# A two-layer decoder on one core: weights converted at other places, and a second bank for the turned probabilities

## Chip, core and metric

One core of one Trainium2 chip runs the whole program in one launch. The metric is device microseconds. A core has TensorE (PE in the profile, with PEld for its weight loads), VectorE (DVE), ScalarE (ACT) and GpSimd (POOL), which run their own instruction streams and wait on one another by semaphores, and SyncE (SP), which issues most DMAs. Matmuls and transposes write PSUM, eight banks of 128x512 f32 each.

## What is computed

`x` and `ctx` are (64, 128, 256) f32: 64 tiles of 128 tokens, 8192 tokens of width 256.

```python
x = x + ssm(layernorm(x))                 # layer 0: scan over 128 tokens, 8 heads of 64, state 128
x = x + cross16(layernorm(x), ctx)        #          16 heads, rotary, keys and values from ctx
x = x + recur(layernorm(x))               #          gated recurrence over the 64 tiles
x = x + self_gqa(layernorm(x))            # layer 1: 16 query heads, 4 key/value heads, s + s @ w_o
x = x + cross1(layernorm(x), ctx)         #          one head of width 256, /sqrt(256)
x = x + moe(layernorm(x))                 #          top 2 of 8 experts by sigmoid(logits + bias),
                                          #          each expert's weight a mean over all its tokens,
                                          #          plus one shared MLP of width 256
```

The recurrence's state goes from tile to tile, and one step of it in layer 0 ends before the next begins. The self attention is `softmax(q k^T / 16) v` for each head, over the 128 tokens of a tile. An expert's factor needs the chosen tokens of the whole input, so no expert output is weighted before all 64 tiles are routed.

## The kernel before, in words

**Phases.** The program is cut into phases with a barrier between them: `start` loads and converts layer 0's weights and computes the decays; `layer0` runs 64 tiles; `between` converts layer 1's weights; `layer1` runs 64 tiles; `route` chooses the experts and converts their weights; `experts` does the shared and the chosen MLPs. In a phase every engine has its own code (`block.tensor`, `block.scalar`, ...).

**Weight jobs.** `weights(pre, scratch, jobs)` gives four functions, for SP, PE, ACT and DVE. A job takes 128 rows of a weight: SP loads them into one of 8 stages, PE transposes 128x128 blocks into bank `j % 4` (L314), ACT copies the first part out (a float32r part, or one half of a plain f32 weight), DVE writes what is left of it (the low part, L344 or L346: weight minus the high part). PE waits for DVE three jobs back. A projection `mm3` then takes three matmuls (L188 to L190) of high and low parts. A narrow job is 128x256, two transposes.

**The loop of layer 1.** `pipeline(eng, lag, step)` calls `step(i)` for 64 + lag values of i; inside a step, `b = i - k` names the tile that each stage works on, and the order of the stages in a step is written out by hand, for each engine apart. So one trip through the loop on an engine is one tile's worth of work, put together from tiles up to six apart on PE. Self attention (`s_`) of a tile goes: layer norm (VectorE's statistics and seed, 11 small steps of a square root's inverse on GpSimd, `newton`, L385, VectorE's norm L1816), `s_transpose` (L1573), `s_project` (L188 to L190, 384 columns), the rotation on VectorE (L1823, L1829), `s_turn_qk` (L1584), `s_heads` on ScalarE (L1720), scores of eight heads into banks 2 and 3 (L709, `scores` 0), maximum (L716), exponentials (L726), then the same banks for the other eight heads (`scores` 1). `turn` g (g = 0 to 3) transposes the probabilities of four heads (L745). All four write bank 4. ScalarE takes turns 0 and 2 out of it (L751), VectorE turns 1 and 3 (`take_by_vector`, L756), both into one count, and each turn waits until the one before is taken. `values` (L779) multiplies them by v, and `s_out` (L188) projects. The one-head attention (`d_`): norm on VectorE (L1816), `d_transpose` into bank 5 (L1597), `d_project`, `d_scores` into bank 6, `d_turn`, `d_values`. The router (`g_`): norm, `g_transpose` (L1628) and `g_logits` (L1634) in bank 7.

VectorE's piece between two steps' statistics is where the engines meet: PE's `d_transpose` waits for VectorE's norm of `d`, which waits for GpSimd's steps, which waits for VectorE's residual.

**Blank rows.** The experts' gather reads a table `pair_rows` in HBM of 11,776 rows of 516 words (512 words of zeros, then a token number and weights), which GpSimd fills with blank rows at the head of `layer1` by four DMAs of 5.9 MB (L1937); its `newton` steps stand behind them in its stream.

**Route.** VectorE computes a one-hot table `t_hot` (L2092) and, later, `t_sums` (L2129). PE's first routing matmuls are at L2023 and L2036; in its stream the jobs `w2` (12 narrow ones) stand before L2023, and `w3` (26) between L2023 and L2036.

Of the kernel before, what the change touches and what calls it, by code (L numbers as in the profile page):

```python
# [26 lines left out]
P = 128  # L27
D = 256
DI = 512
NH = 8  # L30
# [4 lines left out]
DH = 16  # L35
# [25 lines left out]
def constant_table():  # L61
# [29 lines left out]
    "start": """  # L91
        dt_loaded small_loaded halved bias_rows_ready bo2_mm start_state bv_hi bv_lo expA_ready
# [13 lines left out]
        r_tfi r_go r_tg r_xo r_store r_a r_b r_d  # L106
    """.split(),
    "between": """
        w1_load0 w1_load1 w1_load2 w1_load3 w1_load4 w1_load5 w1_load6 w1_load7 w1_scaled w1_tr w1_hi w1_lo b_v b_vrow b_gate l1_small
        l1_wg l1_whi l1_wlo  # L110
# [5 lines left out]
        blank_ready blank s_xo s_u s_h s_x3 s_stats s_aggr s_seed s_rs s_xn s_tr s_hi s_lo s_qkv s_qr s_v s_qtr s_kT  # L116
        s_qT s_sc s_max s_exp s_ptr s_pt s_pv s_rec s_rinv s_rtr s_rT s_o s_ohi s_olo s_proj s_x4
# [5 lines left out]
        w2_load0 w2_load1 w2_load2 w2_load3 w2_load4 w2_load5 w2_load6 w2_load7 w2_scaled w2_tr w2_hi w2_lo  # L123
        w3_load0 w3_load1 w3_load2 w3_load3 w3_load4 w3_load5 w3_load6 w3_load7 w3_scaled w3_tr w3_hi w3_lo
# [11 lines left out]
def decoder(nc, args, xo_dram, cum_dram, table, out):  # L136
# [8 lines left out]
    with ExitStack() as stack:  # L145
# [31 lines left out]
        def pipeline(eng, lag, step):  # L177

            for i in range(lag + 1):
                step(i)  # L180
            with eng.Fori(lag + 1, NB) as i:
                step(i)
            for i in range(NB, NB + lag):
                step(i)
# [40 lines left out]
        WORK, WORKR = 11664, 2560  # L225
# [47 lines left out]
        wpos = [0]  # L273

        def wk(n):
            a = work[:, wpos[0]:wpos[0] + n]
            wpos[0] += n
            assert wpos[0] <= WORK, wpos
            return a
# [11 lines left out]
        def weights(pre, scratch, jobs):  # L291
# [7 lines left out]
            def sync(e):  # L299
                for j, (rows_, n, _, _, _) in enumerate(jobs):  # L300
# [107 lines left out]

        layer0_weights = ExitStack()
        w0r = layer0_weights.enter_context(nc.sbuf_tensor("w0r", [P, 6144], F32R))  # L410
        w0p = layer0_weights.enter_context(nc.sbuf_tensor("w0p", [P, 6144], F32))
        w_out = parts_view(w0r, 0, 4, D)
# [15 lines left out]
        for r in range(2):  # L428
# [5 lines left out]
            for g, (wx, wu) in enumerate(ff):  # L434

                jobs0 += [(wx[r * P:(r + 1) * P, :], D, plain(w_rx, g * D + r * P), 1.0, None),
                          (wu[r * P:(r + 1) * P, :], D, plain(w_ru, g * D + r * P), 0.5, None)]
        jobs0 += [(out_proj[r * P:(r + 1) * P, :], DI, to(w_out, r * P), 1.0, nw_row) for r in range(2)]
# [9 lines left out]
        pdt = [work[:, 8192 + 512 * k:8704 + 512 * k] for k in range(4)]  # L448
        cumT = work[:, 10240:10752]
        q_dtT = work[:, 10752:11264]  # L450
# [3 lines left out]
        PAIRS_OF_X = NB // 2  # L454

# [8 lines left out]
        with phase("start") as block:  # L464
            @block.sync
            def _(e):
                e.dma_start(const[:, :], table[:, 0:C_END]).then_inc(S["const_loaded"], 16)
                e.dma_start(dt_stage, in_proj[DI + XBC:DI + XBC + NH, :]).then_inc(S["dt_loaded"], 16)
                w0[0](e)
# [28 lines left out]
            def _(e):  # L498
# [37 lines left out]
                last.then_inc(S["q_dtT"], 1)  # L536
                w0[1](e, range(PAIRS_OF_X, len(jobs0)))

                e.wait_ge(S["bv_lo"], 1)
                e.wait_ge(S["w0_lo"], len(jobs0))  # L540
# [5 lines left out]
                e.wait_ge(S["p_nd"], 1)  # L546
                e.matmul(dt_bank[:, 0:NT], upper, pdt[3], start=True, stop=True).then_inc(S["p_cum"], 1)
                for k in range(0, NT, P):
                    last = e.matmul(bank[6][:, k:k + P], pdt[3][:, k:k + P], upper, start=True, stop=True)
                last.then_inc(S["p_cumT"], 1)  # L550

            @block.scalar
            def _(e):
# [11 lines left out]
                w0[2](e, range(PAIRS_OF_X, len(jobs0)))  # L565
# [5 lines left out]
                e.activation(pdt[3], pdt[1], ACT.Ln, bias=const[:, C_ONE:C_ONE + 1]).then_inc(S["p_act"], 1)  # L571
                e.wait_ge(S["p_cumT"], 1)
# [1937 lines left out]
```

## Time and profile before

| | |
|---|---|
| time, median of 3 runs | 3503.76 us (3502.93 to 3503.86) |
| the profiled execution | 3505.98 us, of which the span is 3504.2 |
| TensorE's granted clock, mean | 0.957 |
| start, layer 0 (64 tiles) | 87.8 us; 1797.70 us |
| between | 16.50 us |
| layer 1 (64 tiles) | 1085.40 us |
| route; experts | 75.90 us; 440.90 us |
| busy: PE, DVE, ACT, POOL | 89%, 79%, 65%, 44% |

The span is what the trace covers, and the execution's own time is 1.8 us longer. The phases add up to the span, since a barrier stands between them. A phase of 64 tiles costs 64 times its period plus a head and a tail.

### The profile page before, as it was taken

How to read it: one execution, taken by the hardware profiler on the slowest of the kernel's cores; microseconds unless marked ns; L12 is line 12 of the kernel's file. 1: busy time of each engine (PE TensorE's matmuls, PEld its weight loads, DVE VectorE, ACT ScalarE, POOL GpSimd, SP SyncE). 2: the span in 40 equal slices, each digit the busy share in tenths (PEclk: the TensorE clock that was granted, in tenths of full speed). 3: DMA queues.
4: the chain of work that ended last, by engine and by line, in shares of the span. 5: the costliest groups of instructions: out<-in, count | busy, mean ns of one | idle time of the engine just before them, and what ended most of it. 6: DMA issues, size and time to landing. Idle time of an engine off the chain costs nothing. (4 is left out here: it accounts for less than half of the span.)

```text
span 3504.2 us, 95628 instructions
## 1 busy us (share of the span) xinstructions
PE 3118.5 (89%) x27092; PEld 2676.8 (76%) x27093; DVE 2768.9 (79%) x8748; ACT 2282.2 (65%) x8269; POOL 1530.3 (44%) x5116
## 2 busy tenths in 40 slices
PE   6699999999999999999985788888888888499998
PEld 4578888888888888888874677777777777287998
DVE  5588888888888888888872677777777786587776
ACT  3367777777777777777762677777777776133333
POOL 1244455444445444454441355554555454033333
PEclk8699999999999999999996899999999999599999
DMA  5000001001000100000003500000000000122443
GB/s 166 25 31 27 27 28 34 27 27 33 30 27 27 36 27 27 30 33 27 27 24 123 201 15 18 15 18 15 15 18 15 18 15 11 47 89 112 137 137 91
DMA packets 92030, 162.12 MB, mean 46 GB/s; under 512 B 13379, under 2 KB 57584, under 8 KB 91952
## 3 DMA queue, kind: packets, MB, share of 16 engines
q1 hardware_dynamic: 73744, 102.32, 9.7%
q0 software_dynamic: 18208, 58.84, 4.7%
q8 instruction: 39, 0.64, 0.1%
q14 instruction: 39, 0.32, 0.0%
HBM read 102.85 MB, written 61.79 MB: 47 GB/s over the span
## 5 line engine op out<-in xcount | busy, mean ns | idle before, releaser
L385 POOL TENSOR_TENSOR tiny<-tiny 128x1 f32<-128x1 f32 x3456 | 780.3, 226 | 844.4 <-DVE tiny L372 604.0
L726 ACT ACTIVATE work<-bank,att 128x128 f32<-128x128 f32 x2048 | 722.2, 379 | 90.3 <-DVE att L716 84.8
L726 ACT ACTIVATION_READ_ACCUMULATOR work<-bank,att 128x1 f32 x2048 | 447.2, 218 | 0.0
L716 DVE TENSOR_REDUCE att<-bank 128x4 f32<-128x512 f32 x512 | 335.0, 686 | 141.2 <-PE bank L709 139.1
L208 PE MATMUL bank<-work,w0p 128*128 128x128 f32 x3072 | 428.1, 279 | 3.5 <-ACT r_tfi_ L1092 1.8
L208 PEld LDWEIGHTS bank<-work,w0p 128*128 128x128 f32 x3072 | 383.6, 194 | 12.3 <-ACT work L1017 2.6
L188 PE MATMUL bank<-w1r,workr 128*128 (+3 forms) x1058 | 361.0, 341 | 17.1 <-DVE workr L1793 16.6
L745 PE MATMUL bank<-const,work 128*128 128x128 f32 x2048 | 318.1, 278 | 52.5 <-ACT work L751 35.4
L1191 DVE SCALAR_TENSOR_TENSOR work<-work,small 128x127 f32<-128x127 f32 (+2 forms) x1152 | 319.8, 346 | 14.2 <-ACT work L1031 9.5
L190 PE MATMUL bank<-w1r,workr 128*128 (+3 forms) x1058 | 323.0, 305 | 0.0
L189 PE MATMUL bank<-w1r,workr 128*128 (+3 forms) x1058 | 322.5, 305 | 0.0
L709 PEld LDWEIGHTS bank<-work 32*128 32x128 f32 x4096 | 252.3, 188 | 85.7 <-issue 72.1
L709 PE MATMUL bank<-work 32*128 32x128 f32 x4096 | 301.2, 285 | 6.7 <-ACT work L1076 2.5
L745 PEld LDWEIGHTS bank<-const,work 128*128 128x128 f32 x2048 | 237.0, 142 | 84.8 <-ACT work L726 55.8
L385 POOL TENSOR_TENSOR tiny<-tiny,const 128x1 f32<-128x1 f32 x1152 | 257.5, 223 | 90.2
L188 PE MATMUL bank<-w0r,workr 128*128 128x256 f32 (+1 forms) x640 | 215.0, 336 | 45.0 <-DVE workr L1171 41.7
L751 ACT ACTIVATE work<-bank 128x512 f32<-128x512 f32 x384 | 239.7, 624 | 10.9 <-PE bank L745 10.7
L208 PE MATMUL bank<-d_state,w0p 128*128 128x128 f32 x1536 | 237.4, 278 | 0.0
L188 PEld LDWEIGHTS bank<-w1r,workr 128*128 128x128 f32 x1058 | 202.8, 192 | 37.3 <-DVE workr L1793 29.9
L190 PEld LDWEIGHTS bank<-w1r,workr 128*128 128x128 f32 x1058 | 201.7, 191 | 5.8
L189 PEld LDWEIGHTS bank<-w1r,workr 128*128 128x128 f32 x1058 | 203.8, 193 | 2.9
L208 PEld LDWEIGHTS bank<-d_state,w0p 128*128 128x128 f32 x1536 | 205.5, 195 | 0.0
(331 smaller groups left out, 7671.0 us busy)
## 6 DMA issues: line engine op xcount, KB each, us to landing
work<-decay_sums SPq DMA_DIRECT2D x64, 512.0 KB, 3.6
pair_rows<-work POOLq DMA_DIRECT2D x4, 5934.0 KB, 45.1
work<-pair_rows SPq DMA_DIRECT2D x91, 258.0 KB
work<-in_ctx SPq DMA_DIRECT2D x128, 128.0 KB, 2.1
x_res<-in_x POOLq DMA_DIRECT2D x8, 1024.0 KB, 17.0
recurrence_out<-r_xo_ SPq DMA_DIRECT2D x64, 128.0 KB, 1.7
work<-recurrence_out SPq DMA_DIRECT2D x64, 128.0 KB, 2.0
out_dram<-work POOLq DMA_INDIRECT x91
```

The costliest lines, as they stand in the source:

```text
L188: pe.matmul(out_, lhs[0], rhs[0], start=first, stop=False)
L189: pe.matmul(out_, lhs[0], rhs[1], start=False, stop=False)
L190: return pe.matmul(out_, lhs[1], rhs[0], start=False, stop=last)
L208: last = pe.matmul(out_, w[:, k, n0:n0 + P], act[:, k, :], start=first and k == 0, stop=last_ and k == 1)
L385: e.tensor_tensor(out_, a_, b_, ALU.add if b_ is three_halves else ALU.mult)\
L709: mm = e.matmul(sc_banks[g % 2][:, c:c + P], qT[32 * g:32 * g + 32, odd, blk, :], kT[32 * g:32 * g + 32, blk, :], start=True, stop=True)
L716: e.tensor_reduce(a_nm[:, 4 * g:4 * g + 4], sc_banks[g % 2][:, :].rearrange("p (h k) -> p h k", k=P), AX.X, ALU.max, negate=True).then_inc ...
L726: last = e.activation(Pb[g % 2][:, c * P:c * P + P], sc_banks[g % 2][:, c * P:c * P + P], ACT.Exp, bias=a_nm[:, 4 * g + c:4 * g + c + 1], ...
L745: last = e.transpose(pt_bank[:, h * P:h * P + P], Pb[g % 2][:, h * P:h * P + P], ident)
L751: e.activation(PT[:, 512 * g:512 * g + 512], pt_bank[:, :], ACT.Copy).then_inc(S[pre + "_pt"], 1)
L1191: last = e.scalar_tensor_tensor(out=m_acc[:, j, k:P], in0=m_raw_[:, j, 0:P - k], scalar=cw[:, j, CONV - 1 - k:CONV - k], in1=m_acc[:, j, k:P],
```

## The change

Five things move.

1. The phase `between` is gone. Its eight narrow jobs (the recurrence's `uo` and the one-head attention's Wq, Wk, Wv) stand near the end of `start`'s list, which has 42 jobs instead of 34; self attention's weights, the gate and small vectors are loaded and converted in `start` too.
2. The blank rows are stored at layer 0's head, in twelve DMAs (eight of 128x23 pieces of 256 words, four of 128x23 pieces of 4 words), and waited for at GpSimd's end of layer 0.
3. The experts' and the shared weights: 38 narrow jobs of `route` become 15 wide ones at layer 1's head. A wide job has four transposes into one whole bank, one copy of 128x512 and one subtraction of 128x512. PE does all before its loop and waits for the last one; ScalarE does them behind its step 0, VectorE behind its step 1.
4. Turns 0 and 2 keep bank 4 and ScalarE's copies, counted in `s_pt`; turns 1 and 3 go to bank 7, still copied by VectorE, with a count of their own, `s_ptv`. A turn then waits for the turn two before it, not for the one before. The router's transposes and logits move from bank 7 to bank 5, which `d_transpose` and `d_project` use, with two new waits (`d_qk_sb` in `g_transpose`, `g_lg` in `d_transpose`).
5. The order within layer 1's step is another one on PE, ACT, DVE and POOL.

```diff
+    wide = []
+    for x_ in range(E + 2):
+        wide.append((*up_down, [w_gu[...] for s in range(2)]))
...
             @block.tensor
             def _(e):
+                project32(e, bank[5][:, 0:D], d_state[:, :, :], w_uo, 2, 0, D).then_inc(S["b_v"], 1)
+                for j in range(len(wide)):
+                    e.wait_ge(S[f"w2_load{j % 4}"], 32 * (j // 4 + 1))
+                    if j >= 4: e.wait_ge(S["w2_lo"], j - 3)
+                    for o, half in enumerate(halves[j % 4]):
+                        for c in range(2):
+                            last = e.transpose(bank[1 + j % 4][:, (2 * o + c) * P:(2 * o + c) * P + P], half[:, c, :], ident)
+                    last.then_inc(S["w2_tr"], 1)
+                e.wait_ge(S["w2_lo"], len(wide))
...
             def turn(e, b, g):
-                if past(4 * b + g): e.wait_ge(S[pre + "_pt"], 4 * b + g)
+                taken(e, b, g)          # n = 2*b + g//2 of _pt (g even) or of _ptv (g odd)
-                    last = e.transpose(pt_bank[:, h * P:h * P + P], Pb[g % 2][:, h * P:h * P + P], ident)
+                    last = e.transpose(pt_banks[g % len(pt_banks)][:, h * P:h * P + P], Pb[g % 2][:, h * P:h * P + P], ident)
...
             def d_transpose(b):
+                    if past(b - 2): e.wait_ge(S["g_lg"], b - 2)
             def g_transpose(b):
+                    e.wait_ge(S["d_qk_sb"], min(b + 3, NB) if isinstance(b, int) else b + 3)
-                        last = e.transpose(bank[7][:, c * P:c * P + P], g_xn_[:, c * P:c * P + P], ident)
+                        last = e.transpose(bank[5][:, c * P:c * P + P], g_xn_[:, c * P:c * P + P], ident)
...
             @block.gpsimd                                   # layer0's head
+                for k in range(4):
+                    rows_k = slots.rearrange("(s k p) d -> k p s d", k=4, p=P)[k]
+                    for at, n, of in ((0, D, blank), (D, D, blank), (2 * D, 4, blank_end)):
+                        e.dma_start(rows_k[:, :, at:at + n], of.unsqueeze(1).to_broadcast([P, BLANKS // 4, n]))\
+                            .then_inc(S["blank"], 16)
...
             @block.gpsimd                                   # layer1's head
-                for k in range(4):
-                    e.dma_start(slots.rearrange("(s k p) d -> k p s d", k=4, p=P)[k],
-                                blank.to_broadcast([P, BLANKS // 4, ROW])).then_inc(S["blank"], 16)
...
             @block.tensor                                   # route; w3 alike, ahead of the wait for t_sums
-                w2[1](e)
                 e.wait_ge(S["t_hot"], 1)
```

TensorE's stream in layer 1's loop, before, around the end of a step and the head of the next (L745 is `turn` 2 and 3, L1634 `g_logits`, L1613 `d_scores`, L1628 `g_transpose`, L779 `values`, L762 `turn_inverse`, L1584 `s_turn_qk`, L1597 `d_transpose`):

```order
L745 MATMUL bank4<-const,work 128x128 x4
L1634 MATMUL bank7<-w_gate,work 128x8 x2
L745 MATMUL bank4<-const,work 128x128 x4
...
L1613 MATMUL bank6<-work 128x128 x2
...
L1628 MATMUL bank7<-const,work 128x128 x2
...
L779 MATMUL bank1<-work 32x128 x16
L762 MATMUL bank4<-const,att 128x128 x2
L1618 MATMUL bank6<-const,work 128x128
...
L1584 MATMUL bank0<-const,work 128x128 x3
...
L1597 MATMUL bank5<-const,work 128x128 x4
```

The same stretch of TensorE's stream now (L822 is `turn` 1, 2 and 3, L1686 `g_transpose`, L1670 `d_scores`, L856 `values`, L1692 `g_logits`, L1640 `s_turn_qk`):

```order
L822 MATMUL bank7<-const,work 128x128 x4
...
L822 MATMUL bank4<-const,work 128x128 x4
...
L1686 MATMUL bank5<-const,work 128x128 x2
...
L822 MATMUL bank7<-const,work 128x128 x4
L1670 MATMUL bank6<-work 128x128 x2
L856 MATMUL bank1<-work 32x128 x16
L1692 MATMUL bank5<-w_gate,work 128x8 x2
...
L1640 MATMUL bank0<-const,work 128x128 x3
```

Turn 3 now stands in bank 7 with `g_transpose` ahead of it and `g_logits` behind `values`; the second half of the scores, which stood behind turn 0 in the same step, is the first thing of the next, ahead of `s_out` and turn 1.

VectorE's stream between its residual of self attention and the maxima, before (L1867 is the logits' bias, L756 the take of turn 3, L1823 and L1829 the rotation, L1843 the one-head maximum, L1809 `s_join` with its statistics behind it, L1816 the norm of `d`, L716 the maxima):

```order
L1867 TENSOR_TENSOR tab<-bank7,small 128x8
...
L756 COPY work<-bank4 128x512
L1823 TENSOR_TENSOR work<-bank0,const 128x256
...
L1843 TENSOR_REDUCE tiny<-bank6 128x1
...
L1809 TENSOR_TENSOR x_res<-work,x_res 128x256
L399 BN_STATS tiny<-x_res 128x6
...
L1816 TENSOR_SCALAR work<-x_res,tiny 128x256
...
L716 TENSOR_REDUCE att<-bank2 128x4
```

The same place of VectorE's stream now (L833 is the take, L1912 the maximum, L1930 and the first L1885 the router's norm, L1892 the rotation, L1936 the logits' bias, the second L1885 the norm of `d`, L1878 `s_join`):

```order
L833 COPY work<-bank7 128x512
...
L1912 TENSOR_REDUCE tiny<-bank6 128x1
...
L1930 TENSOR_SCALAR tab<-tiny 128x1
...
L1885 TENSOR_SCALAR work<-x_res,tiny 128x256
L1892 TENSOR_TENSOR work<-bank0,const 128x256
...
L1936 TENSOR_TENSOR tab<-bank5,small 128x8
L1885 TENSOR_SCALAR work<-x_res,tiny 128x256
...
L1878 TENSOR_TENSOR x_res<-work,x_res 128x256
```

The norm of `d` stands ahead of `s_join` and its statistics now, but behind the logits' bias; the router's norm stands in front of the rotation, where it stood behind the maxima.

## Rows read from the trace of the kernel before

In the timelines a row is the start in us, the busy us, the engine, the line and its operation, the tiles written and read, how many such instructions stand together, and in brackets the idle time before the first, with what ended it.

**Rows 1.** Busy time by stretch: the phases; clock, DMA share, GB/s last.

```profile
1885.50:1902.00 16.50, 6.58 (x22) 4.21 (x22) 5.39 (x15) 3.65 (x11) 0.00 (x0) 0.50 0.43 113
1902.00:2987.40 1085.40, 923.75 (x8704) 768.82 (x8704) 811.94 (x2881) 773.37 (x3328) 526.87 (x2374) 0.96 0.12 38
2987.40:3063.30 75.90, 36.29 (x138) 21.01 (x138) 48.26 (x106) 12.40 (x39) 0.00 (x0) 0.54 0.18 54
```

**Rows 2.** TensorE's timeline, one step of layer1's loop.

```profile
2217.39 0.63 PE L1597 MATMUL bank<-const,work 128*128 128x128 f32 x4 [1.01 <-DVE work L1816]
...
2228.68 0.63 PE L745 MATMUL bank<-const,work 128*128 128x128 f32 x4 [0.50 <-ACT work L751]
...
2231.90 0.52 PE L1584 MATMUL bank<-const,work 128*128 128x128 f32 x3
...
2233.43 0.63 PE L1597 MATMUL bank<-const,work 128*128 128x128 f32 x4 [1.01 <-DVE work L1816]
...
2233.98 1.16 PE L709 MATMUL bank<-work 32*128 32x128 f32 x16
```

**Rows 3.** ScalarE's timeline, the same step.

```profile
2232.71 0.83 ACT L1720 ACTIVATE work<-bank,const 128x256 f32<-128x256 f32 x2
...
2236.03 0.37 ACT L726 ACTIVATE work<-bank,att 128x128 f32<-128x128 f32 x1 [1.04 <-DVE att L716]
...
2238.70 0.24 ACT L726 ACTIVATION_READ_ACCUMULATOR work<-bank,att 128x1 f32 x1
```

**Rows 4.** VectorE's timeline, the same step.

```profile
2228.24 0.15 DVE L372 TENSOR_SCALAR tiny<-tiny 128x1 int32<-128x1 int32 x1
...
2229.34 0.69 DVE L756 COPY work<-bank 128x512 f32<-128x512 f32 x1 [0.19 <-PE bank L745]
...
2230.98 0.42 DVE L1809 TENSOR_TENSOR x_res<-work,x_res 128x256 f32 x1
...
2232.77 0.41 DVE L1816 TENSOR_SCALAR work<-x_res,tiny 128x256 f32 x1
...
2235.17 1.29 DVE L716 TENSOR_REDUCE att<-bank 128x4 f32<-128x512 f32 x2 [1.66 <-PE bank L709]
...
2236.82 0.16 DVE L1851 RECIPROCAL tiny<-tiny 128x1 f32<-128x1 f32 x1
```

**Rows 5.** GpSimd's timeline, the same step.

```profile
2231.54 0.19 POOL L385 TENSOR_TENSOR tiny<-tiny 128x1 f32<-128x1 f32 x1
```

**Rows 6.** TensorE's timeline, the phase between, its narrow conversions.

```profile
1894.92 2.68 PE L314 MATMUL bank<-const,work 128*128 128x128 f32 x10 [0.18 <-DMA work<-in_L_xattn_Wv]
```

**Rows 7.** VectorE's timeline, layer1's head.

```profile
1912.40 0.41 DVE L1816 TENSOR_SCALAR work<-x_res,tiny 128x256 f32<-128x256 f32 x1 [5.64 <-POOL tiny L385]
...
1966.66 0.42 DVE L1805 TENSOR_TENSOR work<-work,rows 128x256 f32<-128x256 f32 x1 [7.97 <-DMA work<-recurrence_out]
```

**Rows 8.** GpSimd's timeline, layer1's head.

```profile
1903.13 6.01 POOL L1937 DMA_DIRECT2D pair_rows<-work  x4 [0.30 <-POOL work L1933]
```

**Rows 9.** The line that stores the blank rows: its answer.

```profile
L1937 POOL DMA_DIRECT2D pair_rows<-work x4: 1483/1492/1560, 1903.1 to 1907.7; - x4
...
DMA to landing us min/median/max: 20.6/45.1/69.1
```

**Rows 10.** GpSimd's timeline, layer0's head.

```profile
106.44 1.04 POOL L1388 TENSOR_TENSOR work<-work,tiny 128x512 f32<-128x512 f32 x1 [88.28 <-ACT work L1048]
```

**Rows 11.** The page, DMA issues: KB each, us to landing.

```profile
work<-decay_sums SPq DMA_DIRECT2D x64, 512.0 KB, 3.6
```

**Rows 12.** VectorE's timeline, the route phase.

```profile
3004.41 2.03 DVE L2092 TENSOR_TENSOR work<-work 128x1792 f32<-128x1792 f32 x1
...
3047.00 1.07 DVE L2129 TENSOR_REDUCE work<-rows 128x8 f32<-128x512 f32 x1
```

**Rows 13.** TensorE's timeline, the route phase.

```profile
3010.48 6.63 PE L2023 MATMUL bank<-const,work 128*64 128x1 f32 x56
...
3057.09 0.29 PE L2036 MATMUL bank<-work,const 128*128 128x16 f32 x2
```

More of the change, by code:

```diff
@@ L536, in _ @@
                 last.then_inc(S["q_dtT"], 1)
-                w0[1](e, range(PAIRS_OF_X, len(jobs0)))
+                e.wait_ge(S["p_nd"], 1)
+                e.matmul(dt_bank[:, 0:NT], upper, pdt[3], start=True, stop=True).then_inc(S["p_cum"], 1)
+                for k in range(0, NT, P):
+                    last = e.matmul(bank[6][:, k:k + P], pdt[3][:, k:k + P], upper, start=True, stop=True)
+                last.then_inc(S["p_cumT"], 1)
+                w0[1](e, range(PAIRS_OF_X, len(jobs0)))
+                e.wait_ge(S["l1_small"], 9 * 16)
+                for c in range(2):
+                    last = e.transpose(small_bank[:, 2 * NH + c * E:2 * NH + c * E + E], gate_stage[:, c * P:c * P + P],
+                                       ident[0:E, 0:E])
+                last.then_inc(S["q_gate"], 1)
                 e.wait_ge(S["bv_lo"], 1)
+                e.wait_ge(S["b_gate"], 1)
                 e.wait_ge(S["w0_lo"], len(jobs0))
@@ L545, in _ @@
                 last.then_inc(S["bo2_mm"], 1)
[L546 to L550, printed above, removed]
             @block.scalar
@@ L1633, in g_logits @@
                     for c in range(2):
[L1634 removed]
+                        last = e.matmul(bank[5][:, D:D + E], g_T[:, c * P:c * P + P], w_gate[:, c, :],
                                         start=c == 0, stop=c == 1)
@@ L1638, in step @@
                 def step(i):
-                    b = i - 4
+                    b = i - 2
                     if live(b):
-                        d_scores(b)
+                        att1["scores"](e, b, 1)
+                    b = i - 1
+                    if live(b):
+                        s_transpose(b)
+                    b = i - 3
+                    if live(b):
+                        s_out(b)
+                    b = i - 2
+                    if live(b):
+                        att1["turn"](e, b, 1)
+                    b = i - 1
+                    if live(b):
+                        s_project(b)
+                    b = i - 2
+                    if live(b):
+                        att1["turn"](e, b, 2)
                     b = i - 6
@@ L1771, in step @@
                         att1["take"](e, b, 0)
+                    b = i - 4
+                    if live(b):
+                        copy("d_vmm", b + 1, d_v_, bank[6][:, 0:D], "d_v", ("d_pv", b))
                     b = i - 1
@@ L1779, in step @@
                         att1["take"](e, b, 2)
+                    b = i - 6
+                    if live(b):
+                        copy("g_tr", b + 1, g_T, bank[5][:, 0:D], "g_xnT", ("g_sum", b))
+                    b = i - 1
+                    if live(b):
+                        s_values(b)
                     b = i
@@ L1782, in step, with expert_weights @@
                         s_tanh(b)
-                    b = i - 4
-                    if live(b):
-                        copy("d_vmm", b + 1, d_v_, bank[6][:, 0:D], "d_v", ("d_pv", b))
-                pipeline(e, 7, step)
+                def expert_weights():
+                    for j, (_, _, dst) in enumerate(wide):
+                        e.wait_ge(S["w2_tr"], j + 1)
+                        e.activation(dst[0], bank[1 + j % 4][:, :].rearrange("p (o c r) -> p o c r", o=2, c=2), ACT.Copy)\
+                            .then_inc(S["w2_hi"], 1)
+                pipeline(e, 6, step, 0, expert_weights)
             @block.vector
```

385 lines of the change are left out of this document (187 added, 198 removed).

## Prediction

> **What bounds the kernel now.** I read the busy time by stretch first, since the phases add up [rows 1]. Layer 1 takes 1085.40 us with the clock at 0.96 and TensorE busy for 923.75; the phase between takes 16.50 with TensorE busy for 6.58; route takes 75.90 with it busy for 36.29. In the two short phases nothing is saturated: they are chains.
>
> Then the timelines of one step of layer 1. TensorE starts `d_transpose` at 2217.39 and again at 2233.43, so the period is 16.04 us [rows 2]. The reader is to see who ends TensorE's waits in it: 1.01 at `d_transpose` for VectorE's norm (L1816), and 0.50 at turn 3 for ScalarE's take [rows 2]. Two smaller ones of 0.20 and 0.17 stand in the same step. They make 1.9 us of 16.04, and without any TensorE would need about 14.16. The ring that sets the period: `d_transpose`, then the scores, the turns and `s_out` on TensorE, VectorE's residual with its seed, which ends at 2228.24 + 0.15, GpSimd's steps, and the norm, which does not begin before 2232.77, because `s_join` and its statistics (from 2230.98) stand in front of it [rows 4]. GpSimd's steps were done at 2231.54 + 0.19 = 2231.73 [rows 5], so `s_join` costs this ring 1.04 us. The norm releases the transpose at 2233.43.
>
> **The change, part by part.** All is reckoned against the profiled execution's 3505.98 us and moved to the median at the end.
>
> *Start.* Eight narrow jobs come in. In the phase between, five narrow jobs (ten transposes) took 2.68 us of TensorE [rows 6], so 0.54 a job and 8 x 0.54 = 4.3. The casts of self attention's weights and the decays' earlier place in the streams pull against each other; I take them as nothing, between -2 and +3.
>
> *Layer 0's head.* GpSimd issues the blank rows there. Four such DMAs held it for 6.01 us, 1.5 each [rows 8, 9], so twelve hold it for 18 if a DMA's piece size doesn't matter (each again has 128x23 pieces). GpSimd idles 88.28 us up to 106.44 [rows 10], and the phase begins at 87.8, so 18.6 us cover it. The bytes (23.7 MB) landed 69.1 us after their issue at the latest [rows 9]. Beside them run two or three loads of the decays, 3.6 us each when alone [rows 11]. I take +3. Bounds: 0 if these loads stay hidden, and 3 x 8 = 24 if each load waits as the one load of layer 1 does today (below). If the cover were gone, 18 us would show at once.
>
> *Between* goes: -16.5 [rows 1].
>
> *Layer 1's head.* Before, the first norm is at 1912.40, 10.3 us into the phase, 6.01 of it GpSimd's issue [rows 7, 8]; without that it would be at about 4.3. The wide jobs come before TensorE's loop, and VectorE begins them only behind its step 1, hence behind that norm. No wide job is in the trace. Lower bound: twice a narrow job's transposes, 1.07 us. Upper bound: one copy of 128x512 and one of VectorE in a row, as the take of 0.69 us shows [rows 4], if the ring of four banks did not overlap them, 1.4. The ring does overlap them, so I take 1.07: 15 x 1.07 = 16.1, and 4.3 + 16.1 + 1.5 for the last copy and subtraction = 22. Against 10.3 that is +11.7 (up to +17 with 1.4).
>
> *Contention gone.* VectorE waited 7.97 us for the load of the recurrence's output at 1966.66, within 69.1 us of the blank rows' issue (to 1976) [rows 7, 9]. Nothing is stored there now: -8. At the worst the new weight loads cost a part of it again, which I leave in the range.
>
> *The loop.* This is the largest term. With two banks a turn waits for the take two turns back, so the 0.50 goes. The norm of `d` is ahead of `s_join`, so that ring loses the 1.04 us and would allow 15.0. What takes over is the ring of banks 2 and 3. From the rows: one half of the scores begins at 2233.98 and its last exponential ends at 2238.70 + 0.24 [rows 2, 3], 4.96 us. In the new order, counted from the second half's first matmul: exponentials end at 4.96; turn 3 at 5.15; VectorE's take 0.66 later (2228.68 to 2229.34) at 5.81; then take, one-head maximum, the router's norm and the rotation. In the trace take and rotation are 1.29 (2229.34 to 2230.63), maximum with its small step 0.4, the router's norm 0.45 (to 2236.82) [rows 4], so with a hop between 2.2: 8.03. `s_turn_qk` follows at 8.48. From `s_turn_qk` to the end of the heads' copies is 1.64 (2231.90 to 2232.71 + 0.83) [rows 2, 3]: 10.12. The first half of the next scores begins at 10.24, its exponentials end 4.96 later at 15.20, and the second half may start at 15.3. So the period is 15.3 instead of 16.04, with TensorE's own 14.16 below it: -0.74 x 64 = -47. What is late next is VectorE's piece between turn 3's take and the rotation: each 0.1 us there costs 6.4. Bounds: 14.16 from below (-120); above, no gain (0), if the new waits put back what they take.
>
> *Route.* VectorE has `t_hot` at 3004.41 + 2.03 = 3006.44 [rows 12], and TensorE's matmuls for it begin at 3010.48, behind the `w2` jobs: 4.0. It has `t_sums` at 3047.00 + 1.07 = 3048.07 and they begin at 3057.09 [rows 12, 13], behind `w3`: 9.0. Both go: -12.9 with a hop each. The rest of the phase is VectorE's chain and stays.
>
> *Sum.* 4.3 + 3 - 16.5 + 11.7 - 8 - 47 - 12.9 = -65.4. 3505.98 - 65.4 = 3440.6. The median of the runs is 2.2 below the profiled execution, so about **3438 us**.
>
> One rule speaks against the blank rows' new form. The row: every piece before was 2064 bytes, and 23.7 MB took 69.1 us [rows 9]; no row has a piece of 16 bytes in such number. The Trainium skill ("DMA: Bandwidth & Descriptors", section "Specifications") says that a transfer wants at least 512 bytes for the line rate, and that below this the engine does a read-modify-write. By it the 11,776 pieces of 4 words would be dear and the stores would run on longer; by the row the bytes are the same, and the stores end within the first four tiles. As these stores are waited for only at layer 0's end, some 1700 us later, only their neighbours could feel it.
>
> **The rivals.**
>
> *B, the loop gains nothing.* The new waits tie `g_transpose` to `d_qk_sb` and `d_transpose` to `g_lg`, in one bank. The logits' bias stands ahead of the norm of `d` on VectorE, and the logits are behind `values` on TensorE: if they come late, the norm and `d_transpose` wait again, and the ring is as long as today. For it: the trace shows that norm as the engine's meeting point, with 1.01 us waited for. Against: that ring would allow 15.0, which leaves the norm 0.3 us of slack in my count. Then the sum is -65.4 + 47 = -18, so 3485.
>
> *C, the loop comes near TensorE's floor.* If hops that I counted overlap (VectorE's maximum of bank 2 while bank 3 is written, the take beside the last accumulation), the period is 14.2 to 15.0: -67 to -118 for the loop, so 3367 to 3418. For it: TensorE's waits are only 1.9 us, and each is taken away by name. Against: the ring of banks 2 and 3 is made of rows, and that of the norm allows 15.0 and no less unless its hops shrink too.
>
> *D, slower.* GpSimd makes and issues the twelve stores. If it can't run ahead of their drain, because it then holds three times the pieces (35,328), it is held until they are nearly out, 69.1 us and more, not 18. GpSimd's first work in layer 0, at 106.44 now, then comes 50 to 80 us late, and all of layer 0 waits: -65 + 50 to + 80 = -15 to +15, 3489 to 3519. It decides from an issue of about 84 us on. For it: nothing in the trace bounds how many pieces may be outstanding above 11,776. Against: with those, GpSimd went on after 6.01 us while the last byte landed 69.1 us after its issue, so it ran far ahead [rows 8, 9]. The Trainium skill ("DMA: Bandwidth & Descriptors", section "SWDGE vs HWDGE vs iDMA") has GpSimd's software write each descriptor into rings in an SBUF carveout, and rings have an end; the issue of 6.01 us at 11,776 pieces neither shows nor excludes it.
>
> **How the numbers follow.** The forecast (period 15.0 to 15.7) has 0.57, and its own range is 3418 to 3463. B (15.7 to 16.3) has 0.15. C has 0.22. D has 0.06, of which some 0.04 ends slower by over 0.2%, which is about what a measurement of this kernel tells from no change. The range: up to 3485 it takes two thirds of B, down to 3385 (a period of 14.4) more than half of C; left out are about 0.09 below, 0.04 of B and 0.05 of D. Faster 0.94, the same 0.02, slower 0.04.
>
> **What the new profile would show.** No phase between, and start about 92 us. The twelve issues together 18 us, GpSimd's first work in layer 0 near 106 + 4; if it is far later, D. The first `s_transpose` of layer 1 about 22 us into it. A period of 15.3 with TensorE's longest wait at one of the scores for ScalarE's exponentials, and none at turn 3; if its longest wait is at `d_transpose`, B. Route about 63 us. Wrong would make me above all a VectorE whose order in the loop lets the rotation, or the logits, wait for something I hold to be early.

## The result: slower by half a per cent

| | us |
|---|---|
| changed kernel, median of 5 | 3522.08 (3513.41 to 3528.69) |
| before, median of 5 | 3503.76 (3502.93 to 3508.06) |
| ratio | 1.005 (1.0033 to 1.0068) |
| the profiled execution of the changed kernel | 3528.69, of which the span is 3526.9 |

The forecast was 3438. The changed kernel's busy time by phase (same view as [rows 1]: the stretch, its length, each engine's busy time, the clock, DMA share, GB/s):

```profile
0.00:91.20 91.20, 58.87 (x500) 42.04 (x501) 51.42 (x157) 36.07 (x84) 17.00 (x27) 0.91 0.60 178
91.20:1975.60 1884.40, 1682.66 (x14720) 1459.52 (x14720) 1524.91 (x4609) 1298.66 (x4353) 849.19 (x2575) 0.96 0.14 40
1975.60:3022.20 1046.60, 921.48 (x8768) 774.78 (x8768) 835.87 (x2897) 769.74 (x3344) 514.18 (x2368) 0.97 0.07 20
3022.20:3085.80 63.60, 22.20 (x78) 11.75 (x78) 35.95 (x67) 0.62 (x1) 0.00 (x0) 0.50 0.01 2
3085.80:3526.90 441.10, 412.42 (x3026) 382.61 (x3026) 331.81 (x996) 162.00 (x465) 151.81 (x155) 0.97 0.36 112
```

The start is 3.4 us longer, layer 0 is 86.7 us longer (1884.40 against 1797.70), the phase between is gone, layer 1 is 38.8 us shorter [rows 1], route 12.3 shorter: 3.4 + 86.7 - 16.5 - 38.8 - 12.3 + 0.2 for the experts = 22.7, the difference of the spans. So one phase took back more than all the others gave.

GpSimd's timeline at layer 0's head, which answers to [rows 8, 10]:

```profile
92.11 3.01 POOL L1469 DMA_DIRECT2D pair_rows<-extra  x2 [0.30 <-POOL work L1463]
...
96.59 3.05 POOL L1469 DMA_DIRECT2D pair_rows<-extra  x2
146.99 1.48 POOL L1469 DMA_DIRECT2D pair_rows<-work  x1 [47.35 <-issue]
...
152.91 1.48 POOL L1469 DMA_DIRECT2D pair_rows<-extra  x1
195.59 1.48 POOL L1469 DMA_DIRECT2D pair_rows<-extra  x1 [41.21 <-issue]
...
198.57 1.05 POOL L1477 TENSOR_TENSOR work<-work,tiny 128x512 f32<-128x512 f32 x1
```

The reader is to see the brackets with "issue": the engine waited for nothing that the profile names, 47.35 us in front of the sixth store and 41.21 in front of the eleventh, together 88.6. Its first arithmetic in the layer is at 198.57, against 106.44 before [rows 10]. TensorE stands behind it:

```profile
110.37 0.63 PE L934 MATMUL bank<-work 128*128 128x128 f32 x2
199.73 3.65 PE L943 MATMUL bank<-work 128*128 128x64 f32 x16 [88.72 <-POOL work L1477]
```

The loop's period came as forecast: it is 15.34 to 15.35 us. TensorE's timeline, which answers to [rows 2] (L1654 is `d_transpose`, L1640 `s_turn_qk`):

```profile
2315.54 0.60 PE L1654 MATMUL bank<-const,work 128*128 128x128 f32 x4
...
2329.73 0.52 PE L1640 MATMUL bank<-const,work 128*128 128x128 f32 x3 [0.44 <-ACT work L1774]
...
2330.88 0.60 PE L1654 MATMUL bank<-const,work 128*128 128x128 f32 x4
```

`d_transpose` waits for nothing now; the wait of 0.44 is in front of `s_turn_qk`, behind VectorE's rotation and a copy of ScalarE. VectorE's timeline at layer 1's head, which answers to [rows 7]:

```profile
1982.10 0.68 DVE L2005 TENSOR_TENSOR w1r<-bank,w1r 128x512 fp32r<-128x512 f32 x1
...
1997.19 0.69 DVE L2005 TENSOR_TENSOR w1r<-bank,w1r 128x512 fp32r<-128x512 f32 x1 [0.18 <-ACT w1r L1853]
1997.80 0.41 DVE L1885 TENSOR_SCALAR work<-x_res,tiny 128x256 f32<-128x256 f32 x1
```

The fifteen wide jobs take 1982.10 to 1997.88, 1.05 us each. They stand ahead of the first norm (L1885), which comes 22.2 us into the phase.

### The profile page after: what moved, and what is told of

It is laid out like the page before. It is cut to its first block and busy times, and to the rows that moved or that the text cites. A ratio compares the mean times of both kernels' runs of the same rounds, so it can differ in the third digit from the quotient of the medians.

```text
span 3526.9 us, 95395 instructions
## 1 busy us (share of the span) xinstructions
PE 3097.6 (88%) x27092; PEld 2670.7 (76%) x27093; DVE 2780.0 (79%) x8725; ACT 2267.1 (64%) x8246; POOL 1532.2 (43%) x5125
## 5 line engine op out<-in xcount | busy, mean ns | idle before, releaser
L822 PE MATMUL bank<-const,work 128*128 128x128 f32 x2048 | 317.1, 278 | 22.3 <-ACT work L803 18.2
L386 POOL TENSOR_TENSOR tiny<-tiny,const 128x1 f32<-128x1 f32 x1152 | 248.2, 215 | 90.2
L822 PEld LDWEIGHTS bank<-const,work 128*128 128x128 f32 x2048 | 238.6, 142 | 61.9 <-ACT work L803 38.7
L186 PE MATMUL bank<-w1r,workr 128*128 (+2 forms) x802 | 267.8, 334 | 0.4 <-issue 0.2
L186 PE MATMUL bank<-w0r,workr 128*128 128x256 f32 (+1 forms) x640 | 215.1, 336 | 43.9 <-DVE workr L1248 40.5
L206 PE MATMUL bank<-extra,w0p 128*128 128x128 f32 x1536 | 244.1, 282 | 2.8 <-ACT r_tfi_ L1169 1.8
L188 PE MATMUL bank<-w1r,workr 128*128 (+2 forms) x802 | 241.8, 302 | 0.0
L187 PE MATMUL bank<-w1r,workr 128*128 (+2 forms) x802 | 241.7, 301 | 0.0
L206 PE MATMUL bank<-d_state,w0p 128*128 128x128 f32 x1536 | 236.9, 277 | 0.0
L943 PE MATMUL bank<-work 128*128 128x64 f32 x1024 | 135.1, 278 | 90.0 <-POOL work L1477 88.7
L206 PEld LDWEIGHTS bank<-extra,w0p 128*128 128x128 f32 x1536 | 205.0, 194 | 11.3 <-ACT r_tfi_ L1169 2.1
L206 PEld LDWEIGHTS bank<-d_state,w0p 128*128 128x128 f32 x1536 | 205.0, 194 | 0.0
L943 PEld LDWEIGHTS bank<-work 128*128 128x128 f32 x1024 | 130.9, 201 | 90.9 <-issue 89.0
L188 PE MATMUL bank<-w0r,workr 128*128 128x256 f32 (+1 forms) x640 | 196.5, 307 | 0.0
L187 PE MATMUL bank<-w0r,workr 128*128 128x256 f32 (+1 forms) x640 | 196.2, 307 | 0.0
```

What stands on the lines that cost most here:

```text
L186: pe.matmul(out_, lhs[0], rhs[0], start=first, stop=False)
L187: pe.matmul(out_, lhs[0], rhs[1], start=False, stop=False)
L188: return pe.matmul(out_, lhs[1], rhs[0], start=False, stop=last)
L206: last = pe.matmul(out_, w[:, k, n0:n0 + P], act[:, k, :], start=first and k == 0, stop=last_ and k == 1)
L386: e.tensor_tensor(out_, a_, b_, ALU.add if b_ is three_halves else ALU.mult)\
L822: last = e.transpose(pt_banks[g % len(pt_banks)][:, h * P:h * P + P], Pb[g % 2][:, h * P:h * P + P], ident)
```

## The experiments

The theory after the result: GpSimd's issue of stores is held, and the hold is the whole of what went wrong. Rivals: the bytes at that place, the 16-byte pieces, the number of DMAs. Times below are medians, and a ratio is against runs of the kernel before on the same chip, whose medians are 3499.75 to 3502.74. Four kernels (small pieces, that part alone, one bank, `s_join`) have a single run each; their traces are the evidence, and their times are good to some 10 us.

**Whole rows, four DMAs.**

```diff
-        blank, blank_end = wk(D), wk(4)
+        blank = wk(ROW)
...
-                    for at, n, of in ((0, D, blank), (D, D, blank), (2 * D, 4, blank_end)):
-                        e.dma_start(rows_k[:, :, at:at + n], of.unsqueeze(1).to_broadcast([P, BLANKS // 4, n]))
+                    e.dma_start(rows_k, blank.unsqueeze(1).to_broadcast([P, BLANKS // 4, ROW]))
```

> The changed kernel with the blank rows stored at layer 0's head as four DMAs of whole rows of 516 words (11,776 pieces of 2064 bytes, the same bytes), as the kernel before stores them, instead of twelve DMAs with 35,328 pieces. Theory 1, GpSimd can't issue further once some 14,700 pieces are outstanding: no idle time within the four issues, 6 us together, GpSimd's first work in layer 0 near 110 us, and the 88.6 us of idle time within the issues are given back: about 3440. Theory 2, the bytes hold it (23.7 MB at layer 0's head, beside its loads): it is held again, and the time stays near 3522. If the rest of the sum is right, this kernel is at 3438 to 3443.

Measured: 3438.94 us (3436.19 to 3444.92), ratio 0.9822 (0.9806 to 0.9838). GpSimd, and the busy time of layer 0:

```profile
92.99 6.08 POOL L1466 DMA_DIRECT2D pair_rows<-extra  x4 [0.30 <-POOL extra L1462]
111.23 1.04 POOL L1474 TENSOR_TENSOR work<-work,tiny 128x512 f32<-128x512 f32 x1 [12.16 <-ACT work L1125]
```

```profile
91.90:1889.50 1797.60, 1675.53 (x14720) 1453.72 (x14720) 1525.70 (x4609) 1298.65 (x4353) 838.31 (x2566) 0.98 0.12 42
```

No hold, first arithmetic at 111.23, layer 0 at 1797.6 us where the kernel before had 1797.70 [rows 1], with the same bytes stored at the same place. So neither the bytes nor the place cost anything, and the rest of the sum stands: 3439 against the forecast 3438.

**Whole rows, twelve DMAs** (the row ranges 0 to 7, 8 to 15 and 16 to 22 of each quarter). 

> The changed kernel with the blank rows stored at layer 0's head as twelve DMAs, each of whole rows (of every fourth part the rows 0 to 7, 8 to 15 and 16 to 22): as many DMAs as in the changed kernel, but 11,776 pieces. Theory 1, pieces: no hold, 12 issues of 1.5 us, GpSimd's first work near 110 us, about 3440. Theory 3, only some five DMAs may be outstanding: GpSimd is held after the fifth, and the time lies tens of us above that.

Measured: one run, 3429.42 us. Twelve issues in a row:

```profile
91.21 11.05 POOL L1468 DMA_DIRECT2D pair_rows<-extra  x12 [0.30 <-POOL extra L1462]
109.94 1.04 POOL L1476 TENSOR_TENSOR work<-work,tiny 128x512 f32<-128x512 f32 x1 [7.68 <-ACT work L1125]
```

So the number of DMAs alone doesn't hold it. Timed again:

> The kernel with twelve DMAs of whole rows once more, timed in five rounds; its single run was 3429.4 against 3438.9 for four DMAs. If the smaller DMAs are gentler to the decays' loads beside them, it stays near 3430; if that was one run's luck, it lies at 3435 to 3442. The reading beside the time: the end of layer 0 in both traces.

Measured: 3438.23 us (3432.12 to 3440.98), ratio 0.9818 (0.9799 to 0.9838), the same as with four. The single 3429 lay below all five runs; one run of this kernel is good to some 10 us.

**Small pieces only** on GpSimd's side; SyncE stores the zeros at the end of its layer 0 (that edit is not shown).

```diff
-                    for at, n, of in ((0, D, blank), (D, D, blank), (2 * D, 4, blank_end)):
+                    for at, n, of in ((2 * D, 2, blank_end[:, 0:2]), (2 * D + 2, 2, blank_end[:, 2:4])):
```

> The changed kernel with GpSimd storing only the last four words of each blank row at layer 0's head, in eight DMAs of 8-byte pieces (23,552 pieces, 0.2 MB), and SyncE storing the zeros at its end of layer 0 from its own queue. Theory 1, pieces: GpSimd is held once, behind the fifth DMA (14,720 pieces), as in the changed kernel; how long tells what a piece of 8 bytes costs against one of 1024 (47.4 us there). Theory 2, bytes: not held at all. SyncE's stores may lengthen the end of layer 0; the reading is GpSimd's issue alone, not the time.

Measured: 3544.17 us, in which SyncE's stores stall the end of layer 0. GpSimd's issue:

```profile
91.02 7.43 POOL L1475 DMA_DIRECT2D pair_rows<-work  x5 [0.30 <-POOL work L1469]
123.56 4.44 POOL L1475 DMA_DIRECT2D pair_rows<-work  x3 [25.11 <-issue]
```

It is held at the same place, behind the fifth DMA, with 2944 x 5 x 8 bytes, 0.1 MB, asked for. Here are ten microseconds of it and its last stretch (the last two figures of these rows of the windows view are the DMA share and the GB/s):

```profile
97.00:107.00 10.00, 1.88 (x6) 0.57 (x4) 5.75 (x22) 6.04 (x11) 1.45 (x1) 0.80 1.46 6
...
117.00:123.50 6.50, 0.00 (x0) 0.00 (x0) 0.00 (x0) 0.00 (x0) 0.00 (x0) 0.50 0.00 0
```

First the DMA engines are full with 6 GB/s, and at the end none is busy. So bytes don't set where the hold comes. That whole rows in twelve DMAs (11,776 pieces) are not held and eight DMAs of 23,552 pieces are leaves the pieces. Every DMA that was held stood behind five of 2944 pieces, so the runs put the limit between 14,720 and 17,664 pieces and no closer.

**That part of the change alone, on the kernel before.**

```diff
             @block.gpsimd                      # of layer0; the stores at layer1's head are gone
+                for k in range(4):
+                    rows_k = slots.rearrange("(s k p) d -> k p s d", k=4, p=P)[k]
+                    for at, n, of in ((0, D, blank), (D, D, blank), (2 * D, 4, blank_end)):
+                        e.dma_start(rows_k[:, :, at:at + n], ...).then_inc(S["blank"], 16)
```

> The kernel before with one part of the change alone: the blank rows at layer 0's head in twelve DMAs with 35,328 pieces. If the hold of GpSimd's issue is the whole of what went wrong, layer 0 gets 85 to 90 us longer, layer 1's head 14 us shorter (6 of issue, 8 of the wait for the load): 3503 + 88 - 14 = 3577. If the hold needs the other parts of the change (the fuller opening, other tiles in place), it is less than 50 us long.

Measured: 3588.80 us, 89 above the kernel before beside it. GpSimd:

```profile
89.42 7.60 POOL L1395 DMA_DIRECT2D pair_rows<-work  x5 [0.30 <-POOL work L1389]
145.35 7.41 POOL L1395 DMA_DIRECT2D pair_rows<-work  x5 [48.34 <-issue]
195.19 2.96 POOL L1395 DMA_DIRECT2D pair_rows<-work  x2 [42.43 <-issue]
198.17 1.05 POOL L1403 TENSOR_TENSOR work<-work,tiny 128x512 f32<-128x512 f32 x1
```

The holds are 48.34 + 42.43 = 90.8 us, again before the sixth and the eleventh store, so they need no other part of the change. The gain at layer 1's head was smaller than expected. VectorE's timeline there:

```profile
1995.83 0.17 DVE L1882 MEMSET work<- 128x128 f32 x1 [0.90 <-PEq L161]
...
2003.87 0.41 DVE L1829 TENSOR_SCALAR work<-x_res,tiny 128x256 f32<-128x256 f32 x1 [3.31 <-POOL tiny L385]
```

The phase begins 93.6 us later than in the kernel before (its first instruction there is at 1902.19), and the first norm 91.5 later, so the head gave some 2 us and not 6. In the kernel before VectorE's seed was ready at 1906.76, and GpSimd's first step began at 1909.16, right behind its issue [rows 8]: of the 6.01 us of issue only the last 2.4 were waited for. The 8 us of contention behind the first norm are gone (below).

**Spread over four steps.**

```diff
+                def store_blanks(k):            # the three DMAs of quarter k, unchanged
...
                         scale_tokens(b)
+                    if isinstance(i, int) and 1 <= i <= 4:
+                        store_blanks(i - 1)
```

> The changed kernel with its twelve DMAs and their 35,328 pieces unchanged, but issued three at a time (8,832 pieces) behind GpSimd's work of its steps 1 to 4, some 27 us apart. Theory 1, what counts is how many pieces are outstanding when the next DMA is issued: no group is held, each costs GpSimd 4.5 us of issue in a step where it is idle more than that, and the time is that of the kernels with whole rows, 3435 to 3445. Rival, pieces of 16 bytes or the split rows are slow wherever they stand: GpSimd is held again in each group, and the time stays above 3480.

Measured: 3491.02 us (3489.26 to 3495.65), ratio 0.9975 (0.9965 to 0.9985). My theory of outstanding pieces fell here. The holds:

```profile
146.95 3.01 POOL L1470 DMA_DIRECT2D pair_rows<-extra  x2
177.24 1.48 POOL L1470 DMA_DIRECT2D pair_rows<-work  x1 [27.28 <-issue]
...
238.23 1.51 POOL L1470 DMA_DIRECT2D pair_rows<-extra  x1
255.09 1.49 POOL L1470 DMA_DIRECT2D pair_rows<-extra  x1 [15.35 <-issue]
```

The first is inside the second group, before the sixth store, with three DMAs (8832 pieces) outstanding at most, since the third, issued at 117.3, landed at 151.3; the second is before the eleventh, with one. They come at the same count as in the changed kernel, not when much is outstanding. How long they last is told by the landings. The store issued at 148.5 landed 28.4 us after its issue, at 176.9; the next issue begins at 177.24. The one issued at 238.23 landed after 16.5 us, at 254.7; the next begins at 255.09. In the changed kernel the last store ahead of the first hold was issued at 98.1 and landed at most 48.5 us later, at 146.6, and the next issue is at 146.99; ahead of the second hold it is 152.9 + 42.3 = 195.2 and 195.59; in the kernel with small pieces 97.0 + 26.2 = 123.2 and 123.56.

**In fives.**

```diff
+                store_blanks(0, 5)              # the first five stores, at the head
...
+                    if isinstance(i, int) and i == 3:
+                        store_blanks(5, 10)
+                    if isinstance(i, int) and i == 5:
+                        store_blanks(10, 12)
```

> The changed kernel with its twelve DMAs and 35,328 pieces unchanged, but the first five at layer 0's head, the next five behind GpSimd's step 3 (some 80 us later) and the last two behind step 5. The spread kernel showed holds before the sixth and the eleventh store, as in the changed kernel, though hardly any were outstanding there: the count since the start decides where a hold comes (about 14,700 pieces), and it seems to last until what has been issued has landed. Theory 4, so: the holds fall at the sixth and eleventh store again, but nothing is in flight then, so they last next to nothing; the time is 3440 to 3450 (7.4 us of issue in step 3 are partly seen). Rival, each hold costs some 25 to 45 us by itself, whatever is in flight: GpSimd is held twice and the time stays at 3490 or above.

Measured: 3461.41 us (3457.14 to 3467.54), ratio 0.9888 (0.9872 to 0.9905). The second group, and the first store of the third:

```profile
175.72 1.51 POOL L1472 DMA_DIRECT2D pair_rows<-work  x1
177.23 3.01 POOL L1472 DMA_DIRECT2D pair_rows<-extra  x2
```

```profile
244.71 1.52 POOL L1472 DMA_DIRECT2D pair_rows<-extra  x1
```

No hold in any group: the sixth store begins right behind L1485, 78 us after the fifth (which had landed by 97.8 + 49.9 = 147.7). So a hold costs what is still in flight when it comes. The time is 11 us above the top of what I expected. Layer 0 takes 1819 us in this kernel against 1797.6 with whole rows; I put that down to the 7.5 us of issue in step 3 and the stores in the middle of tiles, which no run takes apart.

**One bank again**, in the kernel with four DMAs: `[bank[4], bank[7]]` becomes `[bank[4]]`, with one count.

> The kernel with four DMAs of whole rows, and all four turns of the probabilities in bank 4 again, counted together, with the new order of the loop kept. Theory A, the second bank is what shortens the loop, since turn 3 otherwise waits for ScalarE's take of turn 2: turn 3 starts 0.65 us later, the ring through the rotation gets as much longer, and the period goes from 15.35 to about 16.0, 64 x 0.65 = 42 us above the kernel with four DMAs. Theory B, the new order alone does it: the period stays at 15.35.

Measured: 3480.81 us, 42 above the kernel with four DMAs. TensorE, two `d_transpose` (L1651) and turn 3 between (L822):

```profile
2303.79 0.60 PE L1651 MATMUL bank<-const,work 128*128 128x128 f32 x4
...
2315.01 0.63 PE L822 MATMUL bank<-const,work 128*128 128x128 f32 x4 [0.60 <-ACT work L828]
...
2319.68 0.60 PE L1651 MATMUL bank<-const,work 128*128 128x128 f32 x4
```

The period is 15.89, turn 3 waits 0.60 for ScalarE's take, and the new order alone gives 0.15 us a tile. The second bank gives the rest, 0.54.

**`s_join` ahead of the norm of `d`** on VectorE, in the kernel with twelve DMAs of whole rows.

```diff
+                        s_join(b)
                         normed("d", b, d_xn_, x_res[:, ds(b * D, D)], d_cols, "d_tr", b)
-                        s_join(b)
```

> The kernel with twelve DMAs of whole rows, and on VectorE s_join with its statistics ahead of the norm of d again, as in the kernel before; all else of the new order is kept. Theory A, this ring allows 15.0 and loses 1.04 us to s_join in front of the norm: the period goes to about 16.0, 40 us above. Theory B, in the new order the norm has slack of its own: nothing, or some 10 us at most.

Measured: 3659.45 us, some 221 above, over five times what I expected. `d_transpose` (L1653) and the projection behind it (L206):

```profile
2289.90 0.63 PE L1653 MATMUL bank<-const,work 128*128 128x128 f32 x4 [1.43 <-DVE work L1884]
...
2309.65 0.63 PE L1653 MATMUL bank<-const,work 128*128 128x128 f32 x4 [1.43 <-DVE work L1884]
...
2312.61 2.78 PE L206 MATMUL bank<-work,w1p 128*128 128x128 f32 x16
...
2327.79 0.91 PE L1653 MATMUL bank<-const,work 128*128 128x128 f32 x4 [1.43 <-DVE work L1884]
```

The wait is 1.43, where I had 0.69: the norm moved by the whole of `s_join` and its statistics, 1.78 us, not by 1.04, against 0.35 of slack. That alone would give a period of 16.8 and cost 64 x 1.43 = 92 us. But these periods are 19.75 and 18.14. The windows view shows the rest; the figure ahead of the last two is the granted clock:

```profile
2300.00:2307.00 7.00, 5.94 (x68) 5.01 (x67) 6.16 (x23) 4.48 (x21) 2.41 (x12) 1.00 0.00 0
2307.00:2309.60 2.60, 0.97 (x6) 0.50 (x6) 2.16 (x10) 1.90 (x8) 0.05 (x1) 1.00 0.00 0
2309.65:2312.00 2.35, 2.35 (x21) 1.96 (x22) 0.40 (x2) 0.90 (x2) 1.88 (x8) 0.77 0.15 50
2312.00:2314.00 2.00, 2.00 (x9) 1.82 (x9) 1.67 (x5) 1.45 (x9) 1.09 (x6) 0.50 0.26 72
```

TensorE is busy for 0.97 of 2.60 us, and right behind that the granted clock goes from 1.00 (2.4 GHz) to 0.77 and 0.50 (1.2 GHz), so the matmuls of the next 4 us take up to twice their time. The same stands in the tile behind it, and over stretches of 100 us the clock is 0.84 to 0.86, against 0.97 to 1.00 without the edit. So the wait explains 92 of the 221 us, and the rest goes with the clock. That the longer wait is what brings the clock down is read from this order in one run.

**The rotation earlier** on VectorE, in the same kernel.

```diff
                         att1["take_by_vector"](e, b, 3)
+                        s_rotary(b)
                         d_maximum(b)
                         g_norm(b)
-                        s_rotary(b)
```

> The kernel with twelve DMAs of whole rows, and on VectorE the rotation directly behind the take of turn 3, ahead of the one-head maximum and the router's norm (1.0 us of work). Theory A, the ring take, rotation, transposes, scores, exponentials sets the period of 15.35: it gets 1.0 us shorter, and the period falls until the next ring holds it; the ring through the norm of d allows 15.0, so 64 x 0.35 = 22 us less, or, if that ring has more slack than I counted, down to 14.35, 64 us less. Theory B, another ring sets the period: no change.

Measured: 3417.05 us (3414.40 to 3419.43), ratio 0.9758 (0.9739 to 0.9776), 21 below the kernel that it was made from. The period is 15.07:

```profile
2309.73 0.63 PE L1653 MATMUL bank<-const,work 128*128 128x128 f32 x4
...
2324.80 0.63 PE L1653 MATMUL bank<-const,work 128*128 128x128 f32 x4
```

TensorE waits only twice in it, 0.38 in front of `values` and 0.25 for ScalarE's one-head exponentials, so it has work for some 14.4 of the 15.07 us. The norm of `d` ends 0.25 us ahead of the transposes, as it did before when they waited for it [rows 2, 4].

**Only the router's norm behind it** (take, maximum, rotation, norm).

> The kernel with twelve DMAs of whole rows, and on VectorE only the router's norm behind the rotation; the one-head maximum stays in front of it. The rotation comes 0.6 us earlier instead of 1.0. If the next ring holds the period at 15.07, as in the kernel with the rotation first, the first ring at 15.35 - 0.6 = 14.75 is already below it and the time is the same, 3417; if both edits count alike, 60 in 100 of the 21 us, 3425.

Measured: 3412.10 us (3409.42 to 3414.90), ratio 0.9746 (0.9730 to 0.9762). Its median is the lowest here, but the ratios of this kernel and the last overlap, and they ran on different chips. The period:

```profile
2310.62 0.63 PE L1653 MATMUL bank<-const,work 128*128 128x128 f32 x4
...
2325.66 0.63 PE L1653 MATMUL bank<-const,work 128*128 128x128 f32 x4
```

It is 15.04, so the rotation no longer sets it, as the forecast of these two had it. What does is not shown. The ring through the norm would give 15.0, but TensorE's own work fills 14.4 of it, with no wait at `d_transpose`, and no run moves the one without the other.

## Why the prediction was wrong

**The step that failed** is "GpSimd issues the blank rows there ... so twelve hold it for 18 if a DMA's piece size doesn't matter". The single issues did take 1.5 us, whatever the piece size; twelve in a row from 92.1 would have ended at 110.1, ahead of the 111.23 at which GpSimd's first arithmetic stands in the kernel with four DMAs. What I left out of the sum is that there is a limit in the number of pieces. It stood in the text as rival D, with its place, its price (50 to 80 us) and its result (3489 to 3519), and got 0.06. It came as 88.6 us, and 3438 + 88.6 = 3527 is within 5 us of the median. Two reasons for the low chance were poor. I took the 6.01 us of issue at 11,776 pieces as a sign that GpSimd runs far ahead of the drain, though it bounds nothing above 11,776. And a one-sided unknown of 35,328 pieces against 11,776 known ones deserved far more than 0.06, and a range that reached it. The Trainium skill ("DMA: Bandwidth & Descriptors", section "SWDGE vs HWDGE vs iDMA") says that GpSimd's software writes every descriptor into rings; the holds at equal counts, whatever the bytes, agree with such a ring that has an end. That the ring is the cause is argued, not shown. Nor is it shown where the count begins: GpSimd had issued 23 loads in `start`, eight of them of 1024 pieces, and still the first hold comes after as many stores as the second.

**Even the rival had the mechanism wrong in one point.** It spoke of pieces outstanding. The spread kernel shows a count instead: after five DMAs of 2944 pieces the next does not start until all that was issued has landed, even with one DMA in flight, and in the kernel in fives, with all landed, the same count costs nothing.

**The other rule.** The Trainium skill ("DMA: Bandwidth & Descriptors", section "Specifications") has 512 bytes as the least transfer for the line rate. The traces agree: in the kernel with 8-byte pieces the DMA engines' share is 1.46 at 6 GB/s from 97 to 107 us, and in the changed kernel the third store, of 46 KB in pieces of 16 bytes, lands 6.4 us behind the second, where the second and the fourth, of 2944 KB in pieces of 1024 bytes, take 12.0 and 11.6. Pieces of 1024 bytes cost something against whole rows too: from 97 to 107 us, when of GpSimd's stores only such are under way, the changed kernel moves 271 GB/s with a share of 1.03, the one with four DMAs 374 with 1.01. But nobody waits for the bytes alone; what it adds is the length of a hold.

**The terms that held.** Start: 4.3 forecast, 3.4 measured. Layer 0's head without the hold: +3 forecast, 0 measured in the kernel with four DMAs (1797.6 us). Wide jobs: 1.07 each, measured 1.05; first norm at 22, measured 22.2. This agreement is in part luck. I let the first norm come at 4.3, since GpSimd's issue was gone, and the jobs behind it. But only 2.4 us of that issue had been waited for (above), VectorE's first work on the recurrence's output, which waits for its load, comes 3.8 us into the phase where it came at 2.0, and the jobs stand ahead of the norm. VectorE begins them at 6.5, and the end fits only since I had put 1.5 us behind them. And the 1.05 is not transposes alone, as I had it: TensorE waits 3.5 us within the fifteen jobs for loads of their weights. Contention: -8; from layer 1's first norm (2003.87) to the end of the span (3587.0) the kernel before with that part alone takes 1583.1 us, the kernel before 3504.2 - 1912.40 = 1591.8 [rows 7]: 8.7 less. The loop: 15.3 forecast, 15.34 measured, so -45 for -47. The step with the rotation is shown right: what stands between the take and the rotation does set the period, 0.28 us of it. The next limit measured is 15.07 and 15.04, near the 15.0 of the ring through the norm; that it is this ring and not TensorE's own work of 14.4, which I had at 14.16, is not shown. Layer 1 as a whole gave 38.8, where the terms as measured make 45 + 8.7 - 11.9 = 42. The kernel with four DMAs, with the same loop, gave 42.5 (1042.9 us), so what is missing is no term of the sum; the cause of these 3 us stays open. Route: -12.9 forecast, -12.3 measured.

**The rivals B and C** are excluded by the period of 15.34. What B named, the norm of `d` late behind other work of VectorE, does decide when it is made to happen (`s_join` ahead of it), and at a higher price than mine.

## What to carry to other kernels

Count the pieces of DMAs that GpSimd issues, not their bytes or their number: a row split in three is three times the pieces, and a store that "nobody waits for" can stop the engine that issues it. A resource of which the trace shows only use below a certain point bounds nothing above it, so give the case beyond a fair chance and let the range reach it. In a loop, write down each ring with its length from rows: the two here (15.3 and 15.0) foretold the period of three of four edits to 0.1 us. The fourth failed twice: the work moved ahead of the norm was 1.78 us and not 1.04, and the clock, which no ring has in it, cost more than the wait.

## What the runs showed of the hardware

- GpSimd's plain DMAs of 2944 pieces: the sixth and the eleventh of these stores wait until all issued have landed, and go on 0.3 to 0.4 us after the last landing (41 to 48 us with pieces of 1024 bytes, 25.1 with pieces of 8 bytes, 15 to 27 when spread, nothing when all had landed). DMAs of whole rows, in four or in twelve, are not held; but with 11,776 pieces in all they stay below the 14,720 behind which a hold was seen.
- An issue costs by its pieces: 1.5 us for 2944, 0.92 for about 1000.
- In the kernel with 8-byte pieces the hold outlasts the traffic: no DMA engine is busy from 117.0 to 123.5, but the fifth store counts as landed only at 123.2, and the issue goes on at 123.56. So the hold goes by the landing. Why the landing trails the traffic there stays open.
- With `s_join` ahead of the norm, a stretch of some 2.6 us in which TensorE is busy for about 1.0 is followed, in both periods looked at, by some 4 us with a granted clock down to 0.50 (1.2 GHz). In the kernel before, with waits of 1.01 and 0.50 us in a period [rows 2], the clock over stretches of 100 us is 0.98 to 1.00.
